# Keeping q^T and k^T in SBUF as f32 with heads in 32-partition row groups, instead of bf16 parts laid out through DRAM

## The reference, cut to what matters

```python
qp = q @ Wq.T                       # 16 heads of 16 channels
k, v = jnp.split(latent_kv @ Wkv_expand.T, 2, axis=-1)
scores = jnp.einsum('bhqd,bhkd->bhqk', qh, kh) * inv_sqrt_d
scores = jnp.where(causal, scores, jnp.finfo(scores.dtype).min)
attn = jax.nn.softmax(scores, axis=-1)
out = jnp.einsum('bhqk,bhkd->bhqd', attn, vh)
```

## Time and profile before

| what | value |
|---|---|
| median of 3 runs | 255.47 us (255.03 to 255.53) |
| span of the profiled execution | 253.9 us |
| TensorE matmuls busy | 190.2 us (75%) |
| TensorE weight loads busy | 135.6 us (53%) |
| DVE, POOL, ACT busy | 126.7, 88.4, 76.0 us |
| mean DMA rate | 119 GB/s |

### The profile page before, as it was taken

The page is one execution under the profiler, slowest core; times in us unless marked ns, Lnnn a source line. Parts: engine busy times, 40 slices in busy tenths (PEclk is TensorE's granted clock), DMA queues, the critical chain, the costliest instruction groups (busy, mean ns, idle before and its releaser), DMA issues.

```text
span 253.9 us, 3767 instructions
## 1 busy us (share of the span) xinstructions
PE 190.2 (75%) x1319; PEld 135.6 (53%) x1319; DVE 126.7 (50%) x354; ACT 76.0 (30%) x165; POOL 88.4 (35%) x119
## 2 busy tenths in 40 slices
PE   8589068749983989604899878989899999988000
PEld 3455045426561658403569556868597887766000
DVE  3857027727551794402964727468746665423000
ACT  2133001326630472201651654142203332222000
POOL 7304700124325330000520431000605888867710
PEclk9689759968997699965999979999999999999655
DMA  6419999985799519991011010399511555554556
GB/s 174 135 51 150 118 193 119 158 260 171 186 145 228 221 48 283 146 134 27 3 41 46 3 41 0 105 307 293 177 56 44 83 82 82 79 82 51 62 60 126
DMA packets 32286, 30.28 MB, mean 119 GB/s; under 512 B 2508, under 2 KB 27372, under 8 KB 32268
## 3 DMA queue, kind: packets, MB, share of 16 engines
q1 hardware_dynamic: 28320, 23.26, 45.8%
q0 software_dynamic: 3744, 6.69, 14.2%
q10 hardware_dynamic: 204, 0.10, 0.2%
HBM read 21.15 MB, written 9.83 MB: 122 GB/s over the span
## 4 chain that ended last, share of the span: by engine, by line
PE 32%; DMA 23%; DVE 13%; SPq 11%; issue 8%; POOL 8%; ACT 1%; POOLq 0%; DVEq 0%; ACTq 0%
DMA q_rows<-q_parts_d 10%; DMA out<-y_rows,tok_i 6%; SPq L374 5%; PE m_ps L1332 4%; PE s_ps L1188 4%; PE s_ps L1191 4%; SPq L367 4%; DVE top L803 3%; PE s_ps L1316 3%; DMA q_rows<-shift_t 3%; POOL out L542 2%; PE t_ps L1218 2%; POOL k_parts L530 2%; PE o_ps L1236 2%; POOL odd_d L542 2%
## 5 line engine op out<-in xcount | busy, mean ns | idle before, releaser
L803 DVE TENSOR_REDUCE top<-s_ps 128x2 f32<-128x512 f32 (+1 forms) x48 | 32.2, 687 | 37.6 <-PE s_ps L1191 37.3
L481 POOL TENSOR_SCALAR_AFFINE_SELECT probs<-probs 128x256 f32<-128x256 f32 (+1 forms) x48 | 23.3, 486 | 64.5 <-ACT probs L594 62.8
L594 ACT ACTIVATE probs<-t_ps 128x512 f32<-128x512 f32 x48 | 27.7, 596 | 32.6 <-PE t_ps L1218 29.4
L1188 PE MATMUL s_ps<-mask_b,ident_b 128*128 128x256 bf16 (+1 forms) x48 | 18.6, 388 | 22.3 <-DMA q_rows<-q_parts_d 19.9
L1316 PE MATMUL s_ps<-xn_t,sgu 128*128 128x256 f32 (+1 forms) x96 | 23.5, 385 | 0.0
L1191 PE MATMUL s_ps<-k_rows,q_rows 96*128 96x128 bf16 (+1 forms) x128 | 21.5, 283 | 0.0
L1218 PE MATMUL t_ps<-q_rows,k_rows 99*128 99x256 bf16 x64 | 13.8, 310 | 9.4 <-DMA q_rows<-shift_t 9.1
L1188 PEld LDWEIGHTS s_ps<-mask_b,ident_b 128*128 128x128 bf16 x48 | 5.3, 110 | 27.5 <-issue 21.5
L1316 PEld LDWEIGHTS s_ps<-xn_t,sgu 128*128 128x128 f32 (+1 forms) x96 | 16.5, 182 | 3.4 <-issue 0.6
L1191 PEld LDWEIGHTS s_ps<-k_rows,q_rows 96*128 96x128 bf16 x128 | 13.9, 119 | 5.4 <-issue 4.2
L470 POOL TENSOR_TENSOR k_parts<-rest,k_parts 128x512 bf16<-128x512 f32 x3 | 3.5, 1154 | 36.6 <-DVE k_parts L787 19.4
(11 more groups left out here) (166 smaller groups left out, 382.7 us busy)
## 6 DMA issues: line engine op xcount, KB each, us to landing
k_rows<-k_parts_d SPq DMA_DIRECT2D x24, 128.0 KB, 6.4
q_rows<-q_parts_d SPq DMA_DIRECT2D x24, 128.0 KB, 8.2
wgu_early<-in_w_gu SPq DMA_DIRECT2D x8, 352.0 KB
k_parts_d<-k_parts SPq DMA_DIRECT2D x4, 384.0 KB, 7.1
q_parts_d<-q_parts SPq DMA_DIRECT2D x4, 384.0 KB, 6.9
wdn_early<-in_w_dn SPq DMA_DIRECT2D x8, 176.0 KB
q_rows<-in_w_gu SPq DMA_DIRECT2D x4, 352.0 KB
v_ones<-in_w_gu SPq DMA_DIRECT2D x4, 352.0 KB
```

What stands on the lines that cost most here:

```text
L481: nc.gpsimd.affine_select(out=v, in_=v, compare_op=ALU.is_ge, fill=0.0, base=0, pattern=[[0, v.shape[1]], [1, P]], channel_multiplier=-1). ...
L594: t_ring.emptied(nc.scalar.activation(probs[:, g % 2, u, :], t_ring.bank(job)[:], ACT.Exp, scale=HD ** -0.5), job)
L803: s_ring.emptied(nc.vector.tensor_reduce(dst, src, AX.X, ALU.max), job)
L1188: nc.tensor.matmul(masked, ident_b[:], mask_b[:].unsqueeze(1).to_broadcast([P, len(heads), P]), start=True, stop=False, skip_group_check=True)
```

## The change

The queries and keys stay where the projection puts them, in SBUF, as f32. Their weights are spread first (`wq_wide`, `wk_wide`) so that head 4g + j comes out on partitions 32g to 32g + 15, in the j-th of four column blocks, with zeros on the other 16 partitions; that doubles the columns of the weights, and each projection becomes two jobs. ACT copies a key bank out with a bias that puts 1.0 on row 16 of each group. The maxima go into a zero-filled `top` at the place of row 16; f32 products with a negative identity transpose them, and DVE adds the result into `q_t`. A score product then contracts over 16 rows of one row group and a transposed one over 17, in f32. The DRAM arrays, the splits, SP's stores and loads of rows, and ACT's DMA are gone. `top` has no second copy: batch b + 1's shift is transposed before the next maxima.

The order of score units changes (`S_BESIDE`), so that each stands beside transposed units of another row group, and pairs are issued by `one_after_other`: both waits, the mask, all products of the first unit, all of the second. Batch 0's scores run in six such pairs (`S_FIRST`) with batch 1's projections between them. Batch 2's keys and queries move into batch 0's tail, and batch 3's into batch 1's. The expert weights of the third four have a buffer of their own, and SP issues those of experts 0 to 7 without a wait.

```diff
-Q_PARTS = ((0, 3), (1, 2), (2, 1))
-K_PARTS = ((0, 1, 2), (0, 1), (0,))
-SPLIT_ROWS = 6 * HD
-SHIFT_ROWS = 3
-ROWS = SPLIT_ROWS + SHIFT_ROWS
+
+RG = 32
+
+SHIFT_ROW = HD
...
-    ((("x", 3), ("v", 3)), (), (("k", 3), ("q", 3)), (), ()),
-    ((("gate", 0, 0), ("logits", 0)), (("gu", 0, 0),), (("gate", 0, 1), ("gu", 0, 1)),
-     (("gate", 0, 2), ("gu", 0, 2)), ()),
+    ((("x", 2), ("v", 2)), (("k", 2, 0), ("k", 2, 1)), (("q", 2, 0), ("q", 2, 1)), (), ()),
+    ((("x", 3), ("gate", 0, 0), ("logits", 0)), (("gu", 0, 0), ("v", 3), ("k", 3, 0)),
+     (("gate", 0, 1), ("gu", 0, 1), ("k", 3, 1)),
+     (("gate", 0, 2), ("gu", 0, 2), ("q", 3, 0)), (("q", 3, 1),)),
...
-KEEP_BUSY = {("k", 0): 11, ("q", 0): 3, ("x", 1): 2, ("q", 1): 4, ("s", 0, 0): 10, ("shift", 0): 9}
+KEEP_BUSY = {("k", 0, 0): 11, ("x", 0): 3}
...
+S_BESIDE = ((1, 2, 3), (0, 8, 10), (4, 6, 11), (5, 7, 9))
+
+S_FIRST = ((0, 1), (2, 3), (4, 6), (8, 10), (5, 7), (9, 11))
+FIRST_FILL = ((), (("x", 1),), (("k", 1, 0), ("k", 1, 1)), (("q", 1, 0), ("q", 1, 1)), (("v", 0),), (("v", 1),))
...
-    steps = []
-
-    def proj(b):
-        steps.extend([("k", b), ("x", b), ("q", b), ("v", b)])
-
-    proj(0)
-    proj(1)
-    for u in range(3 * NG):
-        steps.append(("s", 0, u))
-        if u in (1, 4, 7):
-            steps.append(({1: "x", 4: "k", 7: "v"}[u], 2))
-    steps.extend([("shift", 0), ("q", 2)])
+    steps = [("k", 0, 0), ("k", 0, 1), ("x", 0), ("q", 0, 0), ("q", 0, 1)]
+    for units, fill in zip(S_FIRST, FIRST_FILL):
+        steps.extend([("s", 0, u) for u in units])
+        steps.extend(fill)
+    steps.extend([("shift", 0, 0), ("shift", 0, 1)])
...
-                    steps.append(("s", b + 1, 3 * g + u))
+                    steps.append(("s", b + 1, S_BESIDE[g][u]))
...
+            for e in range(2 * EG):
+                load_expert(e)
             for b in range(2):
-                for g in range(NG):
-
-                    t_ring.wait(sp, ("st", b, g, 2))
-                    load_expert(NG * b + g)
-                load_rows(b + 2)
-                if b == 0:
-                    store_parts(3)
...
-            constant(nc.gpsimd.memset(k_rows[SPLIT_ROWS:P].rearrange("r b h t -> r (b h t)").bitcast(F32),
-                                      1.0 + 0x3F80 / 2 ** 23))
+            link(nc.gpsimd.memset(minus_ident[:], 0.0))
+            constant(nc.gpsimd.affine_select(out=minus_ident[:], in_=minus_ident[:], compare_op=ALU.not_equal, fill=-1.0,
+                                             base=0, pattern=[[-1, P]], channel_multiplier=1))
...
+            def copy_k(b, i):
+                job = ("k", b, i)
+                m_ring.wait(act, job)
+                if b == 0 and i == 0:
+                    act.wait_ge(wide_ready, 3)
+                if b >= 2 and i == 0:
+
+                    t_ring.wait(act, ("st", b - 2, NG - 1, 2))
+                m_ring.emptied(nc.scalar.activation(
+                    k_t[:, b % 2, 2 * i:2 * i + 2, :].rearrange("p j t -> p (j t)"), m_ring.bank(job)[:],
+                    ACT.Identity, bias=ones_row[:, 0:1]), job)
...
-            def shift_parts(b):
-
-                for u in (NS - 2, NS - 1):
-                    s_ring.wait_emptied(dve, ("s", b, u))
-                m, sh = top[:, b % 2], shift[:, b % 2]
-                if b >= 2:
-                    m_ring.wait(dve, ("shift", b - 2))
-                link(nc.vector.tensor_scalar(sh[:, :, 0, :], m, -1.0, None, ALU.mult))
-                link(nc.vector.scalar_tensor_tensor(out=shift_rest[:], in0=m, scalar=-1.0, in1=sh[:, :, 0, :],
-                                                    op0=ALU.mult, op1=ALU.subtract))
-                link(nc.vector.tensor_copy(sh[:, :, 1, :], shift_rest[:]))
-                nc.vector.tensor_tensor(sh[:, :, 2, :], shift_rest[:], sh[:, :, 1, :],
-                                        ALU.subtract).then_inc(shift_ready, 1)
+            def add_shift(b):
+
+                for i in range(2):
+                    job = ("shift", b, i)
+                    m_ring.wait(dve, job)
+                    rows = q_t[:, b % 2, 2 * i:2 * i + 2, :].rearrange("p j t -> p (j t)")
+                    m_ring.emptied(nc.vector.tensor_tensor(rows, m_ring.bank(job)[:], rows, ALU.add), job)
...
+            nc.vector.memset(wk_wide[:], 0.0).then_inc(wide_ready, 1)
+            nc.vector.memset(wq_wide[:], 0.0).then_inc(wide_ready, 1)
+            dve.wait_ge(consts, 2)
+            nc.vector.tensor_reduce(ones_row[:], ident[:].rearrange("p (g r) -> p r g", r=RG)[:, SHIFT_ROW:SHIFT_ROW + 1, :],
+                                    AX.X, ALU.add).then_inc(wide_ready, 1)
+            dve.wait_ge(wide_ready, 3)
             stats_of(0)
+            dve.wait_ge(wkv_in, 16)
+            nc.vector.tensor_copy(wk_wide[:, :, :, 0:HD],
+                                  wkv[:, 0:H].rearrange("l (g j d) -> l j g d", g=NG, j=GH)).then_inc(wide_ready, 1)
             normalise(0)
-            split(0, 0, "k")
+            dve.wait_ge(wq_in, 16)
+            for c in range(HC):
+                nc.vector.tensor_copy(wq_wide[:, c, :, :, 0:HD],
+                                      wq[:, c].rearrange("p (g j d) -> p j g d", g=NG, j=GH)).then_inc(wide_ready, 1)
...
+            for n, units in enumerate(S_FIRST):
+                if n in (1, 4):
+                    normalise(1 if n == 1 else 2)
+                for u in units:
+                    maxima(0, u)
+            add_shift(0)
...
-                for m in range(2):
-                    last = nc.tensor.matmul(m_ring.bank(job)[:, S * m:S * m + S], wkv[:, P * m:P * m + P], lat[:, b, :],
+                for n in range(2):
+                    last = nc.tensor.matmul(m_ring.bank(job)[:, S * n:S * n + S],
+                                            wk_wide[:, 2 * i + n].rearrange("l g r -> l (g r)"), lat[:, b, :],
...
+            def scores(b, u, n):
+
+                job = ("s", b, u)
+                if u < 4:
+                    g, j, qt, keys, parts = u, n, 0, P, GH
+                else:
+                    g, j, qt, keys, parts = (u - 4) // 2, 2 * (u % 2) + n, 1, S, 2
+                rows = slice(RG * g, RG * g + HD)
+                ins = nc.tensor.matmul(s_ring.bank(job)[:, keys * n:keys * n + keys],
+                                       q_t[rows, b % 2, j, P * qt:P * qt + P], k_t[rows, b % 2, j, 0:keys],
+                                       start=False, stop=(n == parts - 1), skip_group_check=True)
+                if n == parts - 1:
+                    s_ring.filled(ins, job)
+
+            def turn_shift(b, i):
+                job = ("shift", b, i)
+                if i == 0:
+                    for u in S_BESIDE[-1][-2:] if b else S_FIRST[-1]:
+                        s_ring.wait_emptied(pe, ("s", b, u))
                     if b == 0:
                         pe.wait_ge(consts, 5)
-                    for k in "kq":
-                        pe.wait_ge(rows_in[k][b % 2], 16 * 6 * (b // 2 + 1))
-                bank = s_ring.bank(job)
-                if u < 4:
-                    qt, heads, keys = 0, range(GH * u, GH * u + GH), P
-                    masked = bank[:].rearrange("p (h k) -> p h k", h=GH)
+                m_ring.begin(pe, job)
+                for n in range(2):
+                    for qt in range(QT):
+                        o = S * n + P * qt
+                        last = nc.tensor.matmul(m_ring.bank(job)[:, o:o + P],
+                                                top[:, qt, 2 * i + n].rearrange("p g r -> p (g r)"), minus_ident[:],
+                                                start=True, stop=True)
+                m_ring.filled(last, job)
...
+            def scores_t(b, g, u, n):
+
+                job = ("st", b, g, u)
+                rows = slice(RG * g, RG * g + SHIFT_ROW + 1)
+                k, q = k_t[rows, b % 2], q_t[rows, b % 2]
+                if u < 2:
+                    j, parts = 2 * u + n, 2
+                    ins = nc.tensor.matmul(t_ring.bank(job)[:, S * n:S * n + S], k[:, j, 0:P], q[:, j, :],
+                                           start=True, stop=True)
                 else:
+                    j, parts = n, GH
+                    ins = nc.tensor.matmul(t_ring.bank(job)[:, P * n:P * n + P], k[:, j, P:], q[:, j, P:],
+                                           start=True, stop=True)
+                if n == parts - 1:
+                    t_ring.filled(ins, job)
...
+            def products(job, quarter):
+
+                if job[0] == "s":
+                    one, wide = scores, job[2] >= 4
                 else:
+                    one, wide = scores_t, job[3] < 2
+                if not wide:
+                    one(*job[1:], quarter)
+                elif quarter % 2 == 0:
+                    one(*job[1:], quarter // 2)
+
+            def one_after_other(first, second):
+                for job in (first, second):
+                    if job[0] == "st":
+                        begin_scores_t(*job[1:])
```

(21 more changed lines are left out.)

261 lines of the change are left out of this document (74 added, 187 removed).

## The result

The changed kernel takes **336.23 us** (median of 4 runs, 333.15 to 338.82) against 255.5 for the kernel before (255.03 to 259.0): ratio 1.3152, 95% interval 1.304 to 1.3264. The forecast was 259.1, its range 246 to 284. The prediction was wrong, by 77 us. The profiled execution is the slowest of the four (338.82 us), so its rows lie some 2.6 us above the median.

A forecast was written before the change was run, and what follows sets the result against it. Some 50 us before the experts was taken as chain through DRAM. Stages summed to 156.3, plus 3.1 look-ahead, 159.4 against 155.86: +3.6, 28 us of stall sold for 31 of products; span 257.5, median 259.1, range 246 to 284.

The forecast's parts named there:

- Prices of TensorE's work, at its full clock: Score and transposed products: f32 records 0.216 us per 256 columns, 0.1125 per 128; a unit 0.88 us.
- If products on 16 rows leave it there: Clock rival: TensorE stays at 1.2 GHz, records twice as long, loops cost some 50 us more; chance 0.05.
- The sum, stage by stage: Start to experts: first scores at 13.1, transposed at 35.3, batches 32.6, 38.4, 31.7, 18.3; 156.3 us, plus 3.1 look-ahead.
- The pair: Score unit beside transposed unit: mask 0.15 + products 0.88 + switch 0.3 = 1.33 us.
- mask and switch: Each pair: mask 0.15 us, plus 0.3 for going to 128 rows and back.
- The switch hides: Row-group change slips under mask and products in the pairs; 12.6 us fall away, giving 246.5; chance 0.16.
- The look-ahead: Second unit of a pair starts late, 0.225 us in 14 pairs, 3.1 us in all; bounds 0 and no overlap.
- Strict order: A pair's second unit starts only when the first is nearly done; 0.72 us a pair, 283 us; chance 0.22.
- Loads in a line: Weight loads of both row groups share one path; pairs with 12 or 16 loads lengthen, 9.3 us, 265; chance 0.12.
- Waits: DRAM waits before score units (19.9 us) and transposed scores (9.1) go; DVE's weight copies fit, up to 1 if late.

The follow-up runs named there:

- experiment 1: Changed kernel with every score and transposed product contracted over all 128 rows, shift left at zero, so another output: 281.16 us.
- experiment 10: Changed kernel with 64-row products, pairs in opposite halves from the first stage on, quarters issued in turn, keys held twice by factor copies: 261.49 us.
- experiment 5: Changed kernel with products on 64 rows and units of a pair dealt to opposite halves, shift left at zero: 268.25 us.
- experiment 3: Changed kernel with the products of a pair's two units issued in turn, one quarter of each: 322.91 us.
- 4: Changed kernel with idle 128-row products before each score unit's mask: one gave 348.02 us, three gave 308.07 us.
- 7: Changed kernel with 32 rows per product (added rows zero) and the two units' products issued in turn by quarters: 278.1 us.
- 2: Changed kernel with products on 32 rows in place of 16 and 17, the added rows holding zeros: 309.74 us.
- 8: Changed kernel with products on 64 rows, units dealt as before so 4 of 12 pairs share a half, shift left out: 282.5 us.
- 11: Mask products removed: kernel before 253.64 us; 64-row version with quarters in turn and factor copies 260.93, with first-stage pairs in opposite halves too 255.65.
- experiment 12: 64-row version without masks, pairs in opposite halves from the first stage on, plus twelve idle 128-row products in that stage: 251.28 us.
- 6: Changed kernel with 64-row products, pairs in opposite halves, shift kept, keys held twice with other row groups zero by 32-partition copies: 280.15 us.

## Why the prediction was wrong

- **The step that failed** is the heading of the prices, "Prices of TensorE's work, at its full clock". Every record's length was read at full clock and carried into loops that run at half. The prediction named the case ("If products on 16 rows leave it there, the loops cost some 50 us more"), gave it 0.05, and kept it out of the range. What the runs showed in its place: with 16 and 17 rows the loop of batch 0 is granted 0.53 and takes 39.83 us, and the same records with all 128 rows, although nothing overlaps, are granted 1.00 and take 27.80 (experiment 1). The rows that should have warned were there: in the kernel before, products on 96 and 99 rows stood in every pair, so its clock of 0.84 to 1.0 said nothing on products of 16. A new operation on an eighth of the rows was an unknown with a price of tens of us and needed its bound from both sides: all stages at 1.0, all at 0.5.
- **Its size was too small as well.** 50 us counted the loops only. Against experiment 10, where the clock stays up, the changed kernel's span is 337.1 - 260.2 = 76.9 us longer: 9.6 in the first score stage, 19.5, 17.7 and 19.2 in batches 0 to 2, 12.5 in batch 3, less 1.6 before and after them. Not all of it is the clock: experiment 10 issues the products in turn, and the late second units cost the changed kernel some 6.5 us at full clock already (below), so some 70 us, an estimate, are the clock's.
- **The sum, stage by stage, came out at full clock, in part by luck.** Experiment 10, made of as many products on 64 rows, meets the five stages within 0.9 us each, 1.4 in all. That its time is within 2.4 us (261.49 against 259.1) is luck: no second unit of it starts late (37.83 us behind 37.82 in the first pair of its loop), so the forecast for it is 259.1 - 3.1 = 256.0, and it is 5.5 off, 2.0 of it at the start and 2.5 behind the last stage. The pair is luck too. It takes (20.75 - 4 x 0.79 - 0.5 - 1.1) / 12 = 1.33 us, the forecast's figure, but from two errors that cancel: 0.32 for mask and switch and not 0.45, and 1.01 for the products and not 0.88.
- **The switch hides** (0.16): open in its mechanism, wrong in its time. With 0.15 us for the mask's columns, the switch there and back is left with 0.17 us a pair (on 64 rows), under the 0.21 at which the prediction let this rival win. Yet the pair did not shrink to 1.03, since the products take 0.13 more than summed. Why they do wasn't tested; after a mask there are 0.32 us and not 0.22 from a unit's first record to its second (37.82 to 38.14 us in experiment 10), and without masks that gap stays in some pairs and goes in others.
- **The look-ahead.** No run shows the 0.225 us by which the sum let the second unit start late in 14 pairs, 3.1 us in all; it was the author's estimate. What the runs showed in its place: behind a first unit of eight records the second starts after five of them, 0.56 us late at full clock (experiment 5), 1.02 at half. In the changed kernel it costs some 13 us (experiment 3); at full clock the loop of batch 0 loses 22.91 - 20.75 = 2.2 us, so some 6.5 in three loops, where the sum had 12 x 0.225 = 2.7.
- **Strict order** (0.22) fell: 0.01 to 0.02 us lie between the starts of two units whose first has four records. Line 1116's first record (51.22) also starts ahead of the last three records of line 1156 (51.43, 51.64 and 51.85), which the source issues before it. Experiment 1 shows about what that rival would have looked like: 281.16 us (283 forecast for it).
- **Loads in a line** (0.12) fell: for a pair with 12 loads it asked for 1.2 us of loads and 0.45 beside them, 1.65 in all, and the pair at 46.49 takes 1.40. (Its forecast of 265 left out the 3.1 us of the look-ahead, which the prediction didn't say.)
- **Waits**: right. No stall took the place of the DRAM waits, and the start was 1.4 us late, 0.8 of it a wait for the weight copy on DVE, which the prediction had let fit ahead of the keys.

What is shown of the clock: where the loop of batch 0 had 0.53, more rows at work at the same time brought it to 1.00, by rows in a product (experiments 1 and 5), by three products on 128 rows that nobody reads (4), and, less firmly, by two products overlapping fully (7 against 2 and 3). What isn't settled is how the chip weighs these, and what part short waits of TensorE play beside them: in experiments 2, 8 and 11 the clock holds in one loop or run and falls in another of the same kernel, and experiment 12 filled waits and rows at once. A unit whose four heads lie in four row groups wasn't tried.

The two levels show in the pairs, one of 1.40 us and one of 2.55. Idle time isn't what held the clock down in the changed kernel's loop of batch 0: TensorE was busy 39.83 of 39.83 us at a granted clock of 0.53.

## What to carry to other kernels

When a change makes TensorE's products smaller in rows, price it at both levels of the clock before anything else, and ask what share of the 128 rows works at the same time; a loop with no idle time can still run near 0.5 (39.83 us busy of 39.83 at 0.53). Pad the contraction with zeros where that costs no columns, to 64 rows if two halves can work side by side (the padding itself is free here: 20.75 us for a loop against 20.71 with 32 rows; 128 rows, with nothing side by side, took 27.80), and issue products for different parts of the array in turn, not unit by unit (20.75 us for the loop against 22.91 on 64 rows). And read the granted clock of each stage first: idle products that only cost when they leave the clock where it is can pay when they lift it (three before each mask gave 28 us net of the some 31 us that they take; with one the loops stayed at 0.56 to 0.58).

## What I had not expected of the hardware

- TensorE, busy without a gap for 39.83 us with products mostly on 16 and 17 rows, was granted 0.53; with the same columns on 128 rows it was granted 1.00 in that loop, and in every slice up to the experts' end.
- Zero rows count as rows: the loops of experiments 5 and 6 are both 22.91 us at 1.0.
- Three idle products of 0.216 us before each mask made the kernel 28 us faster; with one it took 12 us more (348.02 in one execution, beside a kernel before that took 263.28), at a clock in the loops of 0.56 to 0.58.
- Two edits that each left the clock of batch 0's loop at 0.53 (39.60 and 35.86 us) gave 1.00 and 20.71 us together.
- ACT copies 32 partitions of 512 columns in 5.53 / 8 = 0.69 us, and 128 partitions by the same instruction in 0.69 us as well (the key copies of the changed kernel, line 513).
